# Routing weights applied to the input of an expert layer instead of its output, in a four-layer language-model tower on one core

## What is computed

```
k = x @ Wx;  q = x @ Wt
h = tanh(q[:, :, None, :] + k[:, None, :, :] + bt)      # U = 64 features
e = exp(einsum('bijq,qo->bij', h, Wa) + ba)
a = e / (sum(e, -1) + 1e-7);  v = a @ x                 # attention, B = 8, T = 512, D = 128

logits = flat @ router_w.T                              # E = 8 experts, best K = 2
dense_w = zeros.at[..., topk_idx].add(softmax(topk_vals))
g = einsum('sd,edh->esh', flat, w_gate)                 # H = 256
u = einsum('sd,edh->esh', flat, w_up)
y = einsum('esh,ehd->esd', silu(g) * u, w_down)
out = einsum('esd,se->sd', y, dense_w)
```

## Time and profile before

| | |
|---|---|
| median of 3 runs | 2193.83 us (2190.69 to 2195.55) |
| the profiled execution | 2191.52 us, its span 2189.7 us |
| busy over the span: PE, DVE, ACT, POOL | 1815.8, 1740.0, 1300.4, 302.1 us |
| attention stage, by its powers (first to last) | 773.47 to 1740.03 us |
| an iteration there | 65.37 us |

### The profile page before, as it was taken

The page is one execution under the profiler, slowest core; times in us unless marked ns, Lnnn a source line. Parts: engine busy times, 40 slices in busy tenths (PEclk is TensorE's granted clock), DMA queues, the critical chain, the costliest instruction groups (busy, mean ns, idle before and its releaser), DMA issues. The chain is left out here.

```text
span 2189.7 us, 31509 instructions
## 1 busy us (share of the span) xinstructions
PE 1815.8 (83%) x11804; PEld 941.9 (43%) x11804; DVE 1740.0 (79%) x4783; ACT 1300.4 (59%) x1355; POOL 302.1 (14%) x360
## 2 busy tenths in 40 slices
PE   6999998897766679999999999999999988764930
PEld 2566755675421124444434444434444553332610
DVE  3777558778777789999999999999999889794632
ACT  1322122232226999999999999999999722010410
POOL 6000013000333000000000000000000000056046
PEclk9998999897778999999999999999999999866965
DMA  5501000000001100000000000000000000032732
GB/s 155 205 1 39 4 15 14 1 1 1 1 0 37 68 1 1 1 1 1 1 1 1 1 1 1 1 1 1 1 1 1 1 1 1 4 149 67 232 94 76
DMA packets 45801, 64.98 MB, mean 30 GB/s; under 512 B 7744, under 2 KB 35920, under 8 KB 44880
## 3 DMA queue, kind: packets, MB, share of 16 engines
q1 hardware_dynamic: 39472, 48.25, 6.6%
q0 software_dynamic: 6176, 14.71, 2.4%
HBM read 37.77 MB, written 23.07 MB: 28 GB/s over the span
## 5 line engine op out<-in xcount | busy, mean ns | idle before, releaser
L2025 ACT ACTIVATE KM<-KM 128x2048 f32<-128x2048 f32 x299 | 580.8, 2049 | 8.0 <-DVE KM L1844 8.0
L1844 DVE TENSOR_SCALAR KM<-big 128x512 f32<-128x512 f32 x1196 | 488.9, 479 | 16.8 <-PE bank L2174 10.7
L2174 PE MATMUL bank<-KM,w_a_wa 128*32 128x512 f32 x2736 | 366.8, 612 | 69.0 <-ACT KM L2025 50.4
L191 POOL TENSOR_TENSOR nrstd<-nrstd,minus_half 128x4 f32<-128x4 f32 (+1 forms) x80 | 78.5, 1005 | 1668.9 <-DVE nrstd L168 1668.7
L2025 ACT ACTIVATE aa_args<-aa_args 128x2048 f32<-128x2048 f32 x149 | 297.5, 2051 | 1.5 <-DVE aa_args L1844 1.5
L1844 DVE TENSOR_SCALAR aa_args<-big 128x512 f32<-128x512 f32 x596 | 244.3, 479 | 1.3 <-PE bank L2174 0.8
L2174 PE MATMUL bank<-aa_args,w_a_wa 128*32 128x512 f32 x1360 | 182.4, 612 | 29.3 <-ACT aa_args L2025 21.0
L2128 PEld LDWEIGHTS bank<-rf_wd,ST 128*128 128x128 f32 x992 | 120.4, 191 | 98.2 <-issue 85.6
L2174 PEld LDWEIGHTS bank<-KM,w_a_wa 128*32 128x32 f32 x2736 | 55.3, 109 | 206.1 <-ACT KM L2025 107.7
L2145 PE MATMUL bank_pair<-XT,rf_wgu 128*128 128x256 f32 x512 | 142.9, 404 | 1.0 <-DVE ST L1915 1.0
L2128 PE MATMUL bank<-rf_wd,ST 128*128 128x128 f32 x992 | 142.8, 287 | 0.4 <-DVE h L1930 0.3
(11 more groups left out here) (440 smaller groups left out, 2856.2 us busy)
## 6 DMA issues: line engine op xcount, KB each, us to landing
queues<-zeros SPq DMA_DIRECT2D x1, 8192.0 KB, 24.0
KM<-queues SPq DMA_DIRECT2D x32, 256.0 KB, 3.7
results<-KM SPq DMA_DIRECT2D x32, 256.0 KB, 3.6
w<-in_w SPq DMA_DIRECT2D x1, 4096.0 KB, 12.5
mf_tv<-in_task_W SPq DMA_DIRECT2D x1, 2048.0 KB, 9.5
la_v<-in_task_W SPq DMA_DIRECT2D x1, 2048.0 KB, 8.6
big<-XN SPq DMA_DIRECT2D x8, 256.0 KB, 2.7
rf_wgu<-in_wgu SPq DMA_DIRECT2D x1, 2048.0 KB, 8.4
```

Source lines behind the costliest of these rows:

```text
L191: self.nc.gpsimd.tensor_tensor(self.m.nrstd[s][:, 0:self.tiles], self.m.nrstd[s][:, 0:self.tiles], self.m.minus_half[:, 0:self.tiles], ALU ...
L1844: last = nc.vector.tensor_scalar(ARG(n, step)[:, cc, :], KU[:, i * T:(i + 1) * T], q, None, ALU.add)
L2025: last = nc.scalar.activation(ARG(n, step), ARG(n, step), ACT.Tanh)
L2174: last = nc.tensor.matmul(m.bank[g][32 * cc:32 * cc + 32, :], w["a_wa"][:, 30 - 2 * k:62 - 2 * k], ARG(n, step)[:, cc, :], start=k == 0, s ...
```

## The change

For tiles 0 to 13 (`weighted`) the routing weights are applied before the up product:

1. SP writes `WT` (128 x 16) to a tensor in memory, `rf_spread`, waits for it, and reads it back spread to all 128 partitions, 2048 numbers to each, into `WB`, a part of `big`. It waits for the weights, for the former use of `WB`, and for each transfer's end.
2. GpSimd multiplies the tile's turned input by two experts' weights per unit: four TENSOR_TENSOR over 128x512 per tile into `XW` (two buffers, `t512b`). The weights are read with 16 numbers from one token to the next. It does so behind the power of the same tile and ahead of that of the next.
3. The up products read `XW` instead of the turned input, and TensorE waits for it (`xw`).
4. The down products of all eight experts are summed in bank 3 without a stop; VectorE adds the bank to `h` once per tile (`ADDED`, 128x2x128) instead of 16 weighted additions.
5. Two steps are biased, 8 and 20, instead of four: VectorE writes the arguments of two more steps per iteration, and ScalarE has two steps fewer of the longer kind.
6. Units begin at 24, 32, 40, 48 instead of 17, 25, 33, 41, with later lags. Tile 14 begins at 25, 29, 33, 37 instead of 17, 25, 33, 37 and is summed as before, like tile 15.

```diff
@@ -1736,7 +1736,7 @@
-BIASED = (8, 15, 17, 24)
+BIASED = (8, 20)
...
-BEGIN, BEGIN_DRAINED, BEGIN_LAST = (17, 25, 33, 41), (17, 25, 33, 37), (9, 13, 17, 21)
+BEGIN, BEGIN_DRAINED, BEGIN_LAST = (24, 32, 40, 48), (25, 29, 33, 37), (9, 13, 17, 21)
+weighted = lambda j: j < LAST - 1
 begin = lambda j, v: (BEGIN_LAST if j == LAST else BEGIN_DRAINED if j == LAST - 1 else BEGIN)[v]
-GATED, UP, TANH, MUL, LIFTED, DOWN, SUM = (0, 1), (2, 3), 3, 7, 8, (6, 7), (14, 15)
-SUM_DRAINED = (12, 13)
-sum_of = lambda j: SUM if j < LAST - 1 else SUM_DRAINED
+GATED, TANH, SUM = (0, 1), 3, (12, 13)
+UP = lambda j: (4, 5) if weighted(j) else (2, 3)
+MUL = lambda j: 8 if weighted(j) else 7
+LIFTED = lambda j: 11 if weighted(j) else 8
+DOWN = lambda j: (10, 11) if weighted(j) else (6, 7)
+ADDED = lambda j: begin(j, EP - 1) + (18 if j < LAST - 2 else 15)
...
+WB = m.big[:, NT * (D + 1) + 2 * PAIRS * T:NT * (D + 1) + 2 * PAIRS * T + E * TOK]
+XW = lambda v: m.t512b[v % 2][:, :].rearrange("p (x s t) -> p x s t", x=2, s=2)
+spread = nc.dram_tensor("rf_spread", (P, 2 * E), F32).ap()
+wt_out, wb_in, xw = sig("wt_out", 16), sig("wb_in", 16), sig("xw", EP)
+SUMMED = lambda j: m.h[:, tile_of(j):tile_of(j) + NC_ + 1:NC_, :]
...
+        for j in range(LAST - 1):
+            sp.wait_ge(w_sb.sem, w_sb.at(j, 1))
+            if j:
+                sp.wait_ge(wb_in.sem, wb_in.at(j - 1, 16))
+            sp.dma_start(spread, WT[:, :, :].rearrange("p s e -> p (s e)")).then_inc(wt_out.sem, 16)
+            sp.wait_ge(wt_out.sem, wt_out.at(j, 16))
+            if j:
+                sp.wait_ge(xw.sem, xw.at(j - 1, EP))
+            sp.dma_start(WB, spread.rearrange("(o t) n -> o (t n)", o=1).broadcast_to([P, E * TOK])).then_inc(wb_in.sem, 16)
...
+            for v in range(EP if weighted(n) else 0):
+                if v == 0:
+                    pool.wait_ge(wb_in.sem, wb_in.at(n, 16))
+                    pool.wait_ge(x_sb.sem, x_sb.at(n, 1))
+                if n or v >= 2:
+                    pool.wait_ge(up_ps.sem, up_ps.at(n, v - 1))
+                nc.gpsimd.tensor_tensor(XW(v), XMT[n % 2][:, 0:TOK].rearrange("p (o s t) -> p o s t", o=1, s=2).broadcast_to([P, 2, 2, P]),
+                                        WB.rearrange("p (t s e) -> p e s t", s=2, e=E)[:, 2 * v:2 * v + 2, :, :], ALU.mult).then_inc(xw.sem, 1)
...
+                if j and weighted(j - 1):
+                    dve.wait_ge(wt_out.sem, wt_out.at(j - 1, 16))
                 nc.vector.tensor_tensor(WT[:, :, :], top.oh[:, 0:2, :], top.oh[:, 2:4, :], ALU.add).then_inc(w_sb.sem, 1)
...
-            for v in begun(j, step, MUL):
+            for v in begun(j, step, MUL(j)):
...
                 nc.vector.scalar_tensor_tensor(TH, TH, 1.0, GATE[:, :, :], ALU.add, ALU.mult).then_inc(a1_sb.sem, 1)
-            for v in begun(j, step, LIFTED):
+            for v in begun(j, step, LIFTED(j)):
...
-            for x in range(2):
-                for v in begun(j, step, sum_of(j)[x]):
+            if weighted(j) and step == ADDED(j):
+                dve.wait_ge(dn.sem, dn.at(j, EP))
+                nc.vector.tensor_tensor(SUMMED(j), SUMMED(j), m.bank[3][:, 0:2 * D].rearrange("p (s d) -> p s d", s=2), ALU.add).then_inc(h_sb.sem, E)
+            for x in range(0 if weighted(j) else 2):
+                for v in begun(j, step, SUM[x]):
...
+                if n >= 3:
+                    units(n - 3, 2 * CS + step)
                 if n >= 2:
                     units(n - 2, CS + step)
...
-                for v in begun(j, step, DOWN[x]):
+                for v in begun(j, step, DOWN(j)[x]):
                     e = 2 * v + x
                     if x == 0:
                         pe.wait_ge(ac_sb.sem, ac_sb.at(j, v + 1))
-                        if v or j:
+                        if weighted(j):
+                            if v == 0 and j:
+                                pe.wait_ge(h_sb.sem, h_sb.at(j, 0))
+                        elif v or j:
                             pe.wait_ge(h_sb.sem, h_sb.at(j, e - 2 * held(j, v)))
...
-                            last = nc.tensor.matmul(OUT(j, v, x)[:, s * D:(s + 1) * D], AC(j, v)[:, x, o:o + P], wd[:, e, a, :],
-                                                    start=a == 0, stop=a == HB - 1)
+                            if weighted(j):
+                                last = nc.tensor.matmul(m.bank[3][:, s * D:(s + 1) * D], AC(j, v)[:, x, o:o + P], wd[:, e, a, :],
+                                                        start=e == s == a == 0, stop=e == E - 1 and a == HB - 1, skip_group_check=True)
+                            else:
+                                last = nc.tensor.matmul(OUT(j, v, x)[:, s * D:(s + 1) * D], AC(j, v)[:, x, o:o + P], wd[:, e, a, :],
+                                                        start=a == 0, stop=a == HB - 1)
...
-                for v in begun(j, step, UP[x]):
+                for v in begun(j, step, UP(j)[x]):
                     e = 2 * v + x
                     if x == 0 and (v or j):
                         pe.wait_ge(ac_sb.sem, ac_sb.at(j, v))
+                    if x == 0 and weighted(j):
+                        pe.wait_ge(xw.sem, xw.at(j, v + 1))
                     for a in range(HB):
-                        last = nc.tensor.matmul(LIFT[:, x, a * TOK:(a + 1) * TOK], wgu[:, e, 1, a, :], XMT[parity][:, 0:TOK], start=True, stop=True)
+                        lifted = XW(v)[:, x, :, :].rearrange("p s t -> p (s t)") if weighted(j) else XMT[parity][:, 0:TOK]
+                        last = nc.tensor.matmul(LIFT[:, x, a * TOK:(a + 1) * TOK], wgu[:, e, 1, a, :], lifted, start=True, stop=True)
```

1 line of the change is left out of this document (removed).

## The result

The changed kernel takes 2196.74 us in the median of 19 runs (2193.45 to 2203.35), the kernel before 2193.83 us in as many (2186.0 to 2199.7). The ratio is 1.0021, with a 95% interval of 1.0013 to 1.0029: slower by 0.2%, some 4.6 us by the ratio (the medians of all runs stand 2.9 apart), where + 23 us was forecast. The profiled execution after took 2197.01 us (span 2195.1), the one before 2191.52 (span 2189.7), which is + 5.4 us in the span. Half of that isn't the change's: the attention stage starts 2.65 us later (at 678.18 in place of 675.53), after stages that the diff doesn't touch. The stage itself, from its first argument instruction to the next layer's first statistics, is longer by 3.2 us (1107.2 in place of 1104.0), and what follows it is shorter by 0.5.

What follows compares the result with a forecast made beforehand. ScalarE bounds the kernel at 65.37 us a period; the change makes VectorE the bound at 66.9. Steady + 21.4, first iterations - 2.6 and drain + 4 give + 23 us on 2193.8, so 2216 us; range 2173 to 2246.

Steps and rivals of the forecast that it cites:

- blocking on VectorE: Attention stage: GpSimd's four multiplications hold up VectorE instructions, 4 x 1.03 = 4.1 us per period, making VectorE the bound; chance 0.60.
- the steady part: Attention stage, iterations 2 to 15: 14 periods longer by 1.5 us each, + 21 us.
- the drain: End of the attention stage: a second unit's tanh, product and lift move there, 0 to 6.5 us, taken as + 4.
- the first iterations: Iterations 0 and 1 of the attention stage: at most two multiplications, only gain, 2 x 1.3 = - 2.6 us.
- VectorE's own work: VectorE per period, undisturbed: 63.4 + 3.2 for arguments - 4.2 for sums + 0.4 for the addition = 62.8 us.
- the upper end: VectorE's loss per period if all four multiplications meet instructions they block: 4 x 1.03 = 4.1 us, the value taken.
- the lower end, 75%: VectorE's loss per period with argument instructions 75% of its time: 4 x 1.03 x 0.75 = 3.1 us.
- the port's rival: Multiplications wait for gaps or fall beside bank reads; ScalarE stays the bound, - 17 us, 2177 us; chance 0.24.
- the part of the range that had been given 0.08: Outcome "same", within about 0.2% (4 us): low end of the forecast and of the late weights, chance 0.08.
- Late weights: Weights through memory reach step 28's up product too late from 11.7 us of transfers on; 2200 to 2228 us; chance 0.08.
- The cover of 8.5 us: From weights done to TensorE reaching step 28's up product: 8.5 us, against 8.7 for transfers and multiplication.
- The powers: GpSimd's small power instructions, one per iteration; standing 66 to 68 us apart was a sign that the forecast is right.

Runs made afterwards that it cites:

- the packed run: Changed kernel with GpSimd's multiplications reading weights from neighbouring elements instead of 64 bytes apart (wrong weights); one execution 2211.33 us, median before 2217.59.
- with placing: Changed kernel with each tile's second to fourth multiplication waiting for the arguments right ahead of a bank-reading VectorE instruction; ratio to before 0.9939, 2201.18 us.
- the later addition: Changed kernel with VectorE's addition of the summed bank one step later (lag 19 instead of 18); ratio to before 1.0034, 2228.22 us.
- weights once: Changed kernel with the weights sent through memory for the first tile only and used by all later tiles; ratio to before 0.9965.

## Why the prediction came out as it did

The direction came out, the mechanism, blocking on VectorE, was right, and the range held the time, which says little, as it reached over both signs. The size was off by 18 us, and the sign came out by luck: it was forecast from the steady part, and that gave + 0.8 us. What is left is the drain's + 4.8 less the first iterations' 2.4, beside a later start that isn't the change's.

*ScalarE.* Two biased steps fewer save 1.3 us: 64.07 us in the two runs in which ScalarE is full with two biased steps. Right.

*VectorE's own work.* 62.8 was reckoned, 62.6 measured. Right.

*The blocking: the step that failed.* The sum took 4 x 1.03 = 4.1 us, and the iterations show 2.7. Two errors of opposite sign are in it. The price of one was too low: a blocked argument instruction takes 1.75 to 1.78 in place of 0.48 us, 1.3 lost of a multiplication of 1.56. The earlier trace rows gave 1.03 of 1.34, and that was right for a packed one: the packed run lost 1.02 of 1.29. The 0.27 us between are the stride's, which the forecast had set against the number instead of adding. And their number was too high: the choice of the upper end took all four as blocking. Even the lower end, 75%, treated the multiplications as falling by chance on VectorE's work. They don't. One that comes in a row of arguments may wait for the next instruction that reads a bank, and then it costs VectorE nothing. Two of four did so. With 1.4 us less loss and 0.2 less work of VectorE a period than forecast, 14 periods give some 22 us, of which the one interval of 66.61 gives back 1.3. That is what is missing from the 23; the drain (+ 0.8 over its term) and the later start of the stage (+ 2.65, not the change's) give a little back. The gain of 1.3 us at ScalarE and the loss at VectorE cancel to 0.04 us a period. The point from which the port's rival was to decide, a loss of 2.57 us in all for a period of 65.37, was the right one to draw, and the case fell on it: the truth lay between the forecast and that rival, in the part of the range that had been given 0.08.

The Trainium skill (SBUF — State Buffer, "Who interferes with whom") states that the shared pair is held for the whole instruction by whoever issues first. The measured loss is 1.3 of 1.56 us here and 1.02 of 1.29 in the packed run, so in both 0.27 us short of the whole instruction. Its half on who comes first isn't what these rows show: the first and the fourth multiplication were there before the arguments they waited for.

The Trainium skill (GPSIMD Engine Reference, section 7, "Performance pitfalls for Q7 kernels") states about one cycle more per element for such steps, an estimated 0.43 us for 512 of them; the packed run shows 0.27 us.

*Late weights.* The transfers were reckoned at 7.3 us; from the weights' end (1195.53) to the first multiplication it is 6.2. Right, a little too dear. The cover of 8.5 us holds where ScalarE sets the period (8.6 with three biased steps and with placing); with VectorE behind it is 6.9 us here, and the multiplication itself was held for 1.6 us behind the arguments. So the wait "near 0" is 2.7 us, and the hold alone decides when it ends, since each first multiplication was ready before line 1942 let it through. This is a second place of the same failed step: the port was reckoned against VectorE alone, and not as a hold on GpSimd and, through it, on TensorE. The forecast also had no term for TensorE's clock, which it had read at 1.00. In the kernel after, one interval stands above VectorE's sum, the 66.61, at a clock of 0.95.

*Ends.* The first iterations: - 2.6 reckoned, - 2.4 measured (- 2.1 and - 0.3). The drain: + 4 taken, + 4.8 measured. The sizes are right; the cause given for the drain wasn't shown.

*What would show it.* Of the signs named, the mean of line 1869 rose (from 480 and 481 ns to 494 and 513, for its two tiles in one iteration), with single instructions over 1 us at the multiplications; VectorE's idle is gone; ScalarE shows waits. The powers stand 65.3 apart, not 66 to 68. A sign against the forecast also came: TensorE's longest wait is for the multiplication, which was to mean late weights. It meant a held multiplication.

## What to carry to other kernels

When work moves to GpSimd beside a busy VectorE, price a collision at the whole GpSimd instruction less some 0.3 us, and count collisions from the order of VectorE's instructions, not from its mix. Then choose the place: gating the GpSimd instruction on the one ahead of a VectorE instruction that reads a bank gave back all of the 1.3 us an iteration. And compare iterations of one trace with each other: here their lengths, their blocks and their granted clocks came in pairs, and a cure that seemed to bring nothing had only worked where the clock was low.

## What the hardware showed that was not expected

Between a multiplication and a running row of argument instructions it isn't settled by these runs who gets through. The first and fourth multiplications waited (3.19 and 3.01 us in the record); the third, in an equal row, did not (1.59 us, and its neighbour 1.78), nor did it in the run with the later addition when it met one (1140.78; its neighbour at 1140.86 took 1.78). The records don't show what differs.

A wait of TensorE was followed by slow products. In the iteration at 1168.93, whose granted clock is 0.97, the timeline of TensorE and the window of its first 3 us behind the wait show

```profile
1205.10 2.04 PE L2179 MATMUL bank_pair<-t512b,rf_wgu 128*128 128x256 f32 x4 [2.70 <-POOL t512b L1857]
1207.07 1.63 PE L2216 MATMUL bank<-KM,w_a_wa 128*32 128x512 f32 x8
...
1205.10:1208.10 3.00, 3.00 (x12) 1.34 (x12) 3.00 (x6) 3.00 (x2) 1.53 (x1) 0.50 0.00 0
```

and after as long a wait in an iteration of clock 1.00

```profile
1335.82 1.10 PE L2179 MATMUL bank_pair<-t512b,rf_wgu 128*128 128x256 f32 x4 [2.84 <-POOL t512b L1857]
1336.85 1.07 PE L2216 MATMUL bank<-aa_args,w_a_wa 128*32 128x512 f32 x8
...
1335.82:1338.82 3.00, 3.00 (x16) 1.48 (x16) 3.00 (x6) 3.00 (x3) 1.54 (x1) 1.00 0.02 5
```

The same products take half as long again to twice as long in the first, at a granted clock of 0.50, which is the lower level of 1.2 GHz. Of the 13 steady intervals after, five are below 1.00, each with a wait of 2.7 us for the multiplication; before, none is. Waits of 2.7 and 2.8 us stand in two intervals at 1.00 too, so the wait alone doesn't decide. The runs in which that wait is 1.6 us or less (ScalarE as the bound, or weights once) stay at 1.00 from the second interval on. The kernel before with two biased steps, which has no multiplication, has four intervals below 1.00, of 66.50 to 66.72 us beside 66.36.

What it costs depends on who is the bound. The four intervals at 0.97 are as long as the others, 65.3 us, since VectorE's sum covers it; in the packed run, whose sum is lower, such an interval is 0.4 us longer. The interval of 66.61 us has 0.95, and there VectorE's sum is only 62.6 + 1.6 = 64.2: it isn't VectorE that stretched it. The runs with the later addition have it again, 66.62 us, and the run with the units one step later has three of 67.2 to 67.3 at 0.95. No run set the clock apart from the wait.
